# A LoRA-and-mixture kernel on one core: its program with a block and without one

## The reference, cut to what matters

```python
def reference(x, itok, W, lora_A, lora_B, W_base, b_base, W_gate, A, B):
    c = x @ W + (x @ lora_A[itok]) @ lora_B[itok]     # x: 8 x 128 x 512, rank 16
    result = c @ W_base.T + b_base
    probs = softmax(c @ W_gate.T)                     # 8 experts
    top_p, top_i = top_k(probs, 2); top_p /= sum(top_p)
    route_w = sum(one_hot(top_i, 8) * top_p[..., None], axis=-2)
    h = einsum('bnd,erd->bner', c, A) * route_w[..., None]
    return x + result + einsum('bner,eor->bno', h, B)
```

## Time and profile before

| what | us |
|---|---|
| median of 3 runs | 67.09 |
| lowest and highest of them | 66.78, 67.29 |
| the profiled execution's own time | 66.92 |
| its span, first to last instruction of the program | 65.2 |
| busy TensorE, VectorE, ScalarE, GpSimd | 61.1, 37.4, 25.8, 17.1 |

### The profile page before, as it was taken

How to read it: one execution, slowest core, us unless ns; L and a number is a source line. 1 busy time by engine, 2 the same in 40 slices (tenths; PEclk the granted TensorE clock), 3 DMA queues, 4 the chain that set the end, 5 groups by cost and what they waited for, 6 DMA issues and landing times.

```text
span 65.2 us, 1280 instructions
## 1 busy us (share of the span) xinstructions
PE 61.1 (94%) x420; PEld 60.1 (92%) x420; DVE 37.4 (57%) x130; ACT 25.8 (40%) x73; POOL 17.1 (26%) x41
## 2 busy tenths in 40 slices
PE   4998999999999999999999999999999999999910
PEld 4997999999999999999999999999999999998900
DVE  0946357699979966010887668970587030684120
ACT  4433739677084670010171456311551021543420
POOL 1005998999884003030030303030000000000000
PEclk9999999999999999999999999999999999999999
DMA  0799999715994002232232332800043000053044
GB/s 0 201 313 331 346 357 394 280 50 194 292 356 149 1 0 46 61 72 62 65 68 64 73 67 45 325 5 0 0 173 148 10 0 0 0 199 123 0 163 159
DMA packets 5048, 8.46 MB, mean 130 GB/s; under 512 B 1057, under 2 KB 1569, under 8 KB 5042
## 3 DMA queue, kind: packets, MB, share of 16 engines
q1 hardware_dynamic: 4514, 7.70, 36.8%
q0 software_dynamic: 384, 0.56, 2.3%
q10 hardware_dynamic: 144, 0.13, 0.6%
HBM read 5.26 MB, written 2.10 MB: 113 GB/s over the span
## 4 chain that ended last, share of the span: by engine, by line
PE 87%; DMA 5%; SPq 1%; ACT 1%; DVE 1%; issue 0%
PE bank L484 22%; PE bank L486 21%; PE bank L485 21%; PE bank L492 9%; PE bank L494 6%; DMA w_raw<-fold_in 5%; PE bank L535 2%; PE bank L551 2%; PE bank L541 1%; ACT wg_hi L278 1%; PE bank L525 1%; DVE y_out L479 1%; SPq L183 1%; SPq L182 1%; PE bank L571 0%
## 5 line engine op out<-in xcount | busy, mean ns | idle before, releaser
L484 PE MATMUL bank<-cl_hi,x_hi 128*128 128x408 f32 x32 | 11.4, 356 | 0.0
L486 PE MATMUL bank<-cl_hi,x_lo 128*128 128x408 f32 x32 | 11.1, 348 | 0.0
L485 PE MATMUL bank<-cl_lo,x_hi 128*128 128x408 f32 x32 | 11.1, 347 | 0.0
L484 PE MATMUL bank<-cr_hi,x_hi 128*128 128x256 f32 x32 | 9.7, 303 | 0.0
L485 PE MATMUL bank<-cr_lo,x_hi 128*128 128x256 f32 x32 | 9.0, 282 | 0.0
L486 PE MATMUL bank<-cr_hi,x_lo 128*128 128x256 f32 x32 | 9.0, 281 | 0.0
L264 POOL CAST cl_hi<-lora_raw 128x64 fp32r<-128x64 f32 x8 | 1.9, 239 | 18.9 <-PE bank L486 18.8
L445 DVE MAX8 top_val<-bank 128x8 f32<-128x8 f32 x8 | 1.4, 170 | 8.6 <-PE bank L535 8.6
L484 PEld LDWEIGHTS bank<-cr_hi,x_hi 128*128 128x128 f32 x32 | 6.1, 190 | 0.1
L484 PEld LDWEIGHTS bank<-cl_hi,x_hi 128*128 128x128 f32 x32 | 6.0, 188 | 0.1
L485 PEld LDWEIGHTS bank<-cr_lo,x_hi 128*128 128x128 f32 x32 | 6.1, 190 | 0.0
(11 more groups left out here) (97 smaller groups left out, 156.5 us busy)
## 6 DMA issues: line engine op xcount, KB each, us to landing
x_raw<-x_t SPq DMA_DIRECT2D x8, 256.0 KB, 4.5
out<-y_out SPq DMA_DIRECT2D x7, 256.0 KB, 2.1
w_raw<-fold_in SPq DMA_DIRECT2D x4, 256.0 KB, 5.6
w_raw<-fold_in SPq DMA_DIRECT2D x3, 324.0 KB, 6.2
bw_rows<-bw_hi SPq DMA_DIRECT2D x16, 40.5 KB, 2.0
lora_raw<-lora POOLq DMA_DIRECT2D x8, 64.0 KB, 4.7
bw_rows<-bw_lo SPq DMA_DIRECT2D x8, 40.5 KB, 2.1
ffn_b_raw<-ffn_b SPq DMA_DIRECT2D x1, 256.0 KB, 8.4
```

The source lines that it names most:

```text
L484: nc.tensor.matmul(out, a_hi, b_hi, start=first, stop=False, skip_group_check=True)
L485: nc.tensor.matmul(out, a_hi, b_lo, start=False, stop=False, skip_group_check=True)
L486: return nc.tensor.matmul(out, a_lo, b_hi, start=False, stop=last, skip_group_check=True)
```

## The change

The block is gone. The five functions get plain names and are called one after the other with the engines, so that each engine's instructions are appended to the same program as the framework's beginning. No instruction of the functions is changed. Line numbers behind L178 fall by 3 to 8.

```diff
-        block = ctx.enter_context(nc.Block())
-
-        @block.sync
-        def _(sp):
+        def sync_program(sp):
...
-        @block.gpsimd
-        def _(pool):
+        def gpsimd_program(pool):
...
-        @block.scalar
-        def _(act):
+        def scalar_program(act):
...
-        @block.vector
-        def _(dve):
+        def vector_program(dve):
...
-        @block.tensor
-        def _(pe):
+        def tensor_program(pe):
...
+        sync_program(nc.sync)
+        scalar_program(nc.scalar)
+        tensor_program(nc.tensor)
+        vector_program(nc.vector)
+        gpsimd_program(nc.gpsimd)
```

## The result

The changed kernel takes 66.06 us (median of 6 executions, 65.64 to 66.42) against 67.19 of the kernel before in the same comparison. The ratio is 0.9845, 95% interval 0.981 to 0.9881: about 1.0 us faster, where 0.38 had been forecast. The ratios in this text compare undisturbed executions alone, while the medians take in all of them. The time fell inside the stated range (66.0 to 67.2) at its edge, but the forecast case, no change that can be told, did not come.

What follows compares the result with a forecast made beforehand. Bound: front edge on SyncE's queue and DMA, solid middle on TensorE, back edge on the last store. 67.09 - 0.38 (end), with 0 for the beginning, = 66.71, rounded to 66.7 us; range 66.0 to 67.2.

Steps and rivals of the forecast that it cites:

- the forecast case: Whole kernel: 0.38 us off the end, nothing off the beginning, 66.7 us, within 1% of before; chance 0.62.
- The bound: Whole kernel: front edge on SyncE's queue and DMA to 5.67 us, solid TensorE middle, back edge on the last store.
- The beginning, 0 to 0.03 us: Program's start: removing one entry branch per engine gains 0.03 us at most, taken as 0.
- The rule that I had set beside it: Program's start: a taken branch outside the instruction window costs a page fetch, making the gain much larger; prediction rejected it.
- The end of the span, 0.38 us: Program's end: of 0.4 us from SyncE's branch at 64.8 to the span's end, 0.02 remains, so 0.38 us go.
- The sum keeps them whole: Outside the span: the 1.72 us before the first and behind the last instruction stay unchanged.
- Rival 1: Behind the program: the slowest engine's housekeeping sets the end, so more comes off, 65.6 to 66.3 us; chance 0.20.
- Rival 2: Behind the program: the span shrinks by 0.38 us but the time does not, 67.1 us; chance 0.11.
- rival 3: TensorE's instruction stream: shifted page ends leave a fetch of 1.04 us bare, slower at 67.75 us; chance 0.07.

Runs made afterwards that it cites:

- the repetition: The changed kernel run once more beside the kernel before on the same chip; 66.16 us against 66.86, ratio 0.9867.
- pool_last: The changed kernel with the last wait for the stores moved from SyncE to GpSimd; 66.71 us, ratio 0.9955 to the kernel before.
- four_wait: The changed kernel with ScalarE, TensorE and VectorE also waiting for the stores at the end, only GpSimd leaving early; ratio 0.9914 to the kernel before.

## Why the prediction was right or wrong

- **The bound** (front edge on SyncE and DMA, solid middle, back edge on the last store): right. Chain, waits and clock after are those of before.
- **The beginning, 0 to 0.03 us**: right. The first issue starts at 0.86 behind 0.07 us, as before, and the count of instructions leaves no room for an entry branch: there was none to remove. The rule that I had set beside it (the Trainium skill, "Runtime: NRT & Kernel Launch", Instruction fetch mechanics) is about a taken branch. It is not refuted here, as the prediction has it, but finds nothing to act on: no fetch was saved. Only the branches at the end that carry a wait are real, and SyncE's costs about 0.1 us.
- **The end of the span, 0.38 us**: mechanism and size are right. From the wait's start to the span's end it is 0.38 us with the block, 0.28 with the meeting alone and 0.02 now. The whole span shows it only roughly: in medians it fell by 0.25 us in the repetition, its scatter being as large as the term.
- **"The sum keeps them whole"**: this is the step that failed. The 1.72 us around the span were carried over unchanged, for want of a row. They depend on which engine leaves the program last, and fell to 1.16 to 1.19. The missing term is 0.5 us, larger than the one that I had summed: 0.37 + 0.5 = 0.9 us, against 0.89 (0.55 to 1.22) in the repetition and 1.0 in the first comparison.
- **Rival 1** was the true case, and its test was stated (around the span "falls to 1.2 or so"). Its idea, that the slowest engine's length sets the end, is what the runs show; its working is not. It took two thirds of 1.72 us, 1.15, which is twice too much, or of half of it, 0.57, which meets the measured 0.5 by luck: the half had no row, and the two thirds came from the ratio 51 to 17 ns of TensorE's and SyncE's semaphore instruction. The runs show TensorE only 0.3 us over SyncE and the whole difference set by GpSimd. For the kernel before this even gives the time: GpSimd's second semaphore instruction starts at 65.1 and takes 0.02 us; with the 1.73 us of `pool_last` that makes 66.85, and the execution took 66.92.
- On what follows the program, the Trainium skill ("Runtime: NRT & Kernel Launch", The launch sequence) lists a barrier that waits for all engines ahead of the resets by each engine. Had such a meeting stood first within the measured time, it would not matter whose arrival is the last; here it matters by up to 0.57 us. So within the measured time no meeting stands first that costs the same whoever comes last. What stands there instead, a part of each engine's own or a hand-over in a fixed order, the runs do not tell.
- **Rival 2** (no gain) and **rival 3** (a bare fetch) did not occur; from 21.00 to 62.01 us TensorE is busy 40.95 of 41.01 us, 40.94 before.
- **The chances**: 0.62 for the forecast against 0.20 for rival 1 leaned on no row but on the lack of one. With a term unknown and of one sign (other engines leaving earlier can hardly cost time), the middle of its bounds would have been the better value than zero.

## What to carry to other kernels

The program's end is paid twice: the meeting of all engines costs 0.3 to 0.4 us of span, and by making all engines leave last it puts the longest of the lengths that follow (GpSimd's) behind the span, 0.5 us more. So let every engine leave as soon as its work is done, and give the last wait, for the stores, to SyncE; by the difference of their lengths GpSimd should be free until about 0.6 us before SyncE leaves (an estimate; the one run has it 2.1 us before). When a change touches the first or last instructions, compare time less span from execution to execution as well as the span: in all but one of these kernels it scatters by about 0.1 us where the span scatters by half a microsecond and more.

## What the runs showed that I had not expected

- What follows the program has a length that depends on the engine which leaves last. Relative to SyncE's 1.16 us (which holds an unknown part that is common to all): VectorE 0.15 us more, ScalarE 0.20, TensorE 0.32, GpSimd 0.57. They overlap. Whether that is each engine's own work or its place in a hand-over is not shown.
- GpSimd without any transfer in the program, leaving last, has 2.22 us outside and in no execution less than 1.80. Not explained.
- The time outside the span does not follow TensorE's clock. One execution of `four_wait` had a mean granted clock of 0.598 and took 101.85 us; 1.45 us of them lay outside its span, as in the others.
- A branch to the next instruction leaves no record, and its removal moved the first issue by nothing; SyncE's branch at the end, with a wait on it, costs some 0.1 us.
